# A basis chunk read as 32 KB in a row from each of 30 matrices, and a scratch laid out by row and type

## The reference

```
w = jnp.einsum('rb,bio->rio', att, basis)          # att [2, 30], basis [30, 512, 512] f32
for r in range(NUM_RELATIONS):
    gate = jax.nn.sigmoid(x_j @ gate_w[r, :, 0])
    msgs.append(gate[:, None] * x_j @ w[r])
msg = jnp.where((edge_type == 0)[:, None], msgs[0], msgs[1])
agg = jax.ops.segment_sum(msg, row, num_segments=x.shape[0])
return agg + x @ root + bias
```

## Time and profile before

| | us |
|---|---|
| median of 3 runs | 1989.06 |
| lowest and highest | 1987.30 and 1990.79 |
| the profiled execution, device time | 1988.88 |
| its span from first to last instruction | 1986.8 |

### The profile page before, as it was taken

The page is one execution under the profiler, slowest core; times in us unless marked ns, Lnnn a source line. Parts: engine busy times, 40 slices in busy tenths (PEclk is TensorE's granted clock), DMA queues, the critical chain, the costliest instruction groups (busy, mean ns, idle before and its releaser), DMA issues.

```text
span 1986.8 us, 23275 instructions
## 1 busy us (share of the span) xinstructions
PE 1867.5 (94%) x7728; PEld 891.8 (45%) x7728; DVE 798.5 (40%) x1918; ACT 625.1 (31%) x1200; POOL 8.0 (0%) x27
## 2 busy tenths in 40 slices
PE   5898886999999899999999999999999999977998
PEld 3555554633334344444444444454444444433443
DVE  7887775242111541110112223354544445483122
ACT  2555555146761241111111000132322323374000
POOL 1000000000000000000000000000000000000000
PEclk9999999799999779999999999999999999998999
DMA  7999988701000330100001111800000000021011
GB/s 186 266 251 254 238 214 248 286 1 38 1 0 1 132 153 0 43 1 1 21 0 43 43 32 34 337 0 6 22 6 22 6 22 17 6 74 48 21 53 43
DMA packets 46809, 157.52 MB, mean 79 GB/s; under 512 B 8747, under 2 KB 10691, under 8 KB 38247
## 3 DMA queue, kind: packets, MB, share of 16 engines
q1 hardware_dynamic: 42160, 142.27, 23.9%
q10 hardware_dynamic: 4534, 13.78, 1.9%
HBM read 120.38 MB, written 35.65 MB: 79 GB/s over the span
## 4 chain that ended last, share of the span: by engine, by line
PE 79%; DMA 7%; DVE 6%; issue 3%; DVEq 3%; ACT 2%; POOL 0%; ACTq 0%; POOLq 0%; SPq 0%
PE psum L1241 30%; PE psum L1227 30%; PE psum L1460 6%; DMA hs<-in_L_gnn_basis 3%; PE psum L1310 3%; PE psum L1363 2%; DMA adj<-in_L_gnn_basis 2%; PE psum L1411 2%; DMA hs<-in_L_gnn_Wim 2%; PE psum L1144 1%; PE psum L1165 1%; PE psum L1381 1%; DVE hs L597 1%; DVEq L585 1%; DVEq L598 1%
## 5 line engine op out<-in xcount | busy, mean ns | idle before, releaser
L1241 PE MATMUL psum<-hs,adj 128*128 128x512 f16 x2880 | 642.2, 380 | 0.8 <-DVE hs L722 0.8
L1227 PE MATMUL psum<-wb,xt 128*128 128x512 f32 x1152 | 508.9, 600 | 4.8 <-DVE hs L850 2.7
L1241 PEld LDWEIGHTS psum<-hs,adj 128*128 128x128 f16 x2880 | 279.8, 98 | 353.4 <-issue 36.2
L1227 PEld LDWEIGHTS psum<-wb,xt 128*128 128x128 f32 x1152 | 218.4, 192 | 272.9 <-issue 270.8
L1001 ACT ACTIVATE adj<-hs,pbias 128x512 f32<-128x512 f32 x216 | 134.5, 708 | 88.5 <-PE psum L1310 88.5
L1034 ACT ACTIVATE ua<-ua 128x512 f32<-128x512 f32 x60 | 37.8, 631 | 335.3 <-DVE ua L864 187.7
L801 DVE TENSOR_TENSOR vt<-psum,adj 128x512 f32<-128x512 f32 x24 | 16.6, 692 | 271.9 <-PE psum L1227 271.9
L1460 PE MATMUL psum<-hs,adj 128*128 128x512 f32 x288 | 123.8, 592 | 0.0
L1026 ACT ACTIVATE lnst<-lnst,bcol 128x1 f32<-128x1 f32 x36 | 10.6, 295 | 286.7 <-DVE lnst L781 283.4
L858 DVE SCALAR_TENSOR_TENSOR vt<-vt,scl,psum 128x512 f32<-128x512 f32 x60 | 44.8, 747 | 133.7 <-PE psum L1241 133.5
L849 DVE SCALAR_TENSOR_TENSOR vt<-psum,scl,hs 128x512 f32<-128x512 f32 x60 | 45.1, 751 | 122.0 <-ACT hs L1070 121.8
(11 more groups left out here) (223 smaller groups left out, 1891.2 us busy)
## 6 DMA issues: line engine op xcount, KB each, us to landing
hs<-in_L_gnn_basis SPq DMA_DIRECT2D x38, 960.0 KB, 12.1
adj<-in_L_gnn_basis SPq DMA_DIRECT2D x26, 960.0 KB, 14.8
aw_scratch<-xt ACTq DMA_DIRECT2D x12, 768.0 KB, 9.9
adj<-aw_scratch SPq DMA_DIRECT2D x1, 9216.0 KB, 35.9
x_scratch<-adj SPq DMA_DIRECT2D x24, 256.0 KB, 2.1
hs<-x_scratch SPq DMA_DIRECT2D x24, 256.0 KB, 2.6
ts_scratch<-adj SPq DMA_DIRECT2D x1, 4608.0 KB, 20.4
as_scratch<-adj SPq DMA_DIRECT2D x1, 4608.0 KB, 31.4
```

The costliest lines, as they stand in the source:

```text
L1227: x = pe.matmul(psum[:, bank, :], xt[:, i, k, :], w[:, k, :], start=first and k == 0, stop=last and k == 3)
L1241: x = pe.matmul(psum[:, i % 2 + (4 * half if own else 0), :], adj[:, m, j, P * i:P * i + P], hs[:, t, half, j, :], start=n == 1 or (own an ...
```

## The change

Five places change. The chunk's address: partition 4b + j now holds rows 16c + 4j to 16c + 4j + 3 of matrix b, so the four partitions of one matrix read 16 rows, 32 KB in a row, and the matrices are 1 MB apart. Before, the 120 partitions read 8 KB each at places 256 KB apart. The column order of attw: type t and quarter j are in column 2j + t instead of 4t + j (a stride of 2 in the output of the same four VectorE instructions). The scratch's shape: [512 rows, 2 types, 512] instead of [8, 128, 512]. The scratch write: the 8 partitions of one v, now in the order (j, t), go to four places of 4 KB (both types of one row) that are 16 KB apart, instead of eight places of 2 KB that are 256 KB apart. The read-back picks type t out of rows of 4 KB.

```diff
-        wc_dram = [nc.dram_tensor(f"comb{k}_scratch", [8, P, D], F32, kind="Internal").ap() for k in range(2)]
+        wc_dram = [nc.dram_tensor(f"comb{k}_scratch", [4 * P, 2, D], F32, kind="Internal").ap() for k in range(2)]
...
-        bases = [ins[f"L1_gnn_basis{l + 1}"].rearrange("b (j i) o -> (b j) (i o)", j=4) for l in range(2)]
-        combs = [wc_dram[l].rearrange("j (c q) o -> q j c o", q=4) for l in range(2)]
+        bases = [ins[f"L1_gnn_basis{l + 1}"].rearrange("b (c j i) o -> c b j (i o)", j=4, i=4) for l in range(2)]
+        combs = [wc_dram[l].rearrange("(c j q) t o -> c q j t o", j=4, q=4) for l in range(2)]
...
-                sp.dma_start(basis[basis_of(n)][0:120, :], bases[l][:, c * (4 * D):(c + 1) * (4 * D)]).then_inc(basis_in[basis_of(n)], 16)
+                sp.dma_start(basis[basis_of(n)][0:120, :], bases[l][c]).then_inc(basis_in[basis_of(n)], 16)
...
-                    sp.dma_start(combs[l][q, :, c, :], mixed[n % 4][32 * q:32 * q + 8, :]).then_inc(comb_out[n % 4], 16)
+                    sp.dma_start(combs[l][c, q], mixed[n % 4][32 * q:32 * q + 8, :]).then_inc(comb_out[n % 4], 16)
...
-                    sp.dma_start(wb[:, t, :, :], wc_dram[l][4 * t:4 * t + 4].rearrange("j p o -> p j o")).then_inc(weights["l1" + "ab"[l]], 16)
+                    sp.dma_start(wb[:, t, :, :], wc_dram[l].rearrange("(k p) t o -> t p k o", p=P)[t]).then_inc(weights["l1" + "ab"[l]], 16)
...
-                    x = dve.tensor_scalar(attw[0:120, l, 4 * t:4 * t + 4], attm[0:120, :], attc[0:120, l, t:t + 1], None, ALU.mult)
+                    x = dve.tensor_scalar(attw[0:120, l, t:8:2], attm[0:120, :], attc[0:120, l, t:t + 1], None, ALU.mult)
```

## The result

The changed kernel takes **2003.5 us** (median of 6 runs, 1999.7 to 2007.2), the kernel before 1991.6 (6 runs, 1987.3 to 1998.1; three of them are the runs shown ahead of the prediction). The ratio is 1.0052 with a 95% interval of 1.0033 to 1.0070: slower by some 10 us. The prediction, 1981 us, was to be faster by 8, so it has the wrong sign; its range, to 2004, holds the result by half a microsecond. The profiled execution took 1999.86 us, its span is 1997.7.

The account below looks back on a forecast made before the run. It took VectorE's pace, then late basis loads from about 150 us, to bound the building stage. Quicker loads gave -8 us, the other parts 0 or inside the 2 us left: 1988.88 to 1981 us, range 1977 to 2004.

Parts of the forecast that it names:

- What bounds the stage: Building stage, first 330 us: VectorE sets the pace until about 150 us, then late basis loads; at most 10 us to save.
- Step 1: Basis loads: new addresses, 32 KB in a row per matrix, are read faster, so fewer loads are late: -8 us.
- Step 2: Scratch writes: perhaps four engines instead of eight; 0 with quick loads, else 23 to 35 us more on these engines.
- part 1: Same as Step 1: the basis loads are read faster, -8 us.
- the third case: Same as The writes on four engines decide: scratch writes cost +8 to +35 us, taken at +12; chance 0.20.
- Step 3: SP's issuing of loads and scratch writes: at most 0.51 us each, SP busy 2.4 of 4.8 us; 0 to +2 us.
- SP case: SP's issuing becomes the bound from 1.1 us per scratch write; +50 us, 2039 us; chance 0.04.
- Step 4: Reading back the scratch, four loads of 1 MB in 2 KB pieces: nobody waits, cost 0, cover 28 us.
- The writes on four engines decide: Building stage: loads no quicker, scratch writes cost 0.36 to 0.54 us more per chunk; 2001 us, 1997 to 2024; chance 0.20.
- Nothing happens: Basis loads: engines stay in step, 2 MB apart, and read as slowly as before; 1989 us, within 4; chance 0.27.
- The reads get slower: Basis loads: matrices 1 MB apart read at a tenth less rate, 0.43 us per chunk, 28 over all; 2017 us; chance 0.04.

Follow-up runs that it names:

- the quick kernels: Kernel before with each basis load filling 128 partitions, 1 MB in a row (0.9953), or cut into partitions 0 to 111 and 112 to 119 (0.9949).
- the three delay runs: Kernel before with SP kept busy by semaphore increments: ten behind each load (0.9986), ten ahead of each load (0.9996), five behind each scratch write (1.0005).
- The cut at 112: Kernel before with each basis load issued as two transfers, partitions 0 to 111 and 112 to 119: 0.9949, 1981.8 us.

## Why the prediction was wrong, step by step

- **What bounds the stage** held. Late loads against VectorE's pace is what the floor of the quick kernels shows: "at most 10 us" to be won came out as 9.4 and 10.2 (0.9953 and 0.9949 of 1993 us). Of these the forecast took 8.
- **Step 1, the loads read faster (-8), failed.** It named "120 places of 8 KB, 256 KB apart" as what the slow loads have and the others haven't. But rows 8 and 9 differ from rows 7 in a second thing as well, the number of partitions: their transfers fill all 128, the basis loads 120. The prediction compared rows that differ in two things and chose the one that the change touches. The contiguous read into 120 partitions (15.2 GB/s) and into 128 (23.7) settle it. So the sentence that rows 7 against rows 8 agree with a slow pitch does not hold either. In place of -8 the new loads gave +3 to +6 us (1.0028, 1.0016).
- **Step 2, the writes on four engines**: the count came true (1025 small packets fewer, 1020 forecast). "0 if part 1 comes true" held too, 0.9957 against 0.9953 with quick loads. With slow loads the third case asked +8 to +35 and took +12; measured are 1.0012 and 1.0021, **2 to 4 us**. The engines' rate was not the hard limit that the sum took: in the changed kernel a busy engine gave 16.1 instead of 15.1 GB/s, with the new writes alone 16.0. That this made the cost small is argued, as it is not known what raised the rate.
- **Step 3, SP's issuing**, was sized too low: 0.51 us at most for either, measured 0.58 per write and 0.91 per load; the nearest rows, loads of the scratch with equal shapes, were no bound. SP is busy 3.4 us of a chunk, not 2.4. The lateness was under-rated too: SP was late for 17 of 60 loads, where the forecast had some of the last ten. That it is covered held as far as it was tried: the three delay runs show no cost of either half of it, and both halves together were not run. The SP case (from 1.1 us per write) was far.
- **Step 4**, reading back: landing 5.0/6.2/7.4 us and, as said, no wait of TensorE or ScalarE for it.
- **The cases.** "The writes on four engines decide", 0.20, comes nearest: 2001 forecast, 2003.5 measured, and waits from 91 us on, its sign. But only some 3 of the 10 us are its own, so that the time it names was met by luck. "Nothing happens" had the right view of the rate (still 15 to 16) and the wrong reason. "The reads get slower" got its sign only: not a lower rate, no 28 us.
- **Open** is what the new loads cost. It is not their addresses in the sense of places and pitch, as those of old shape show. The trace has their issue 0.58 us longer and the quickest landing at 7.7 to 8.1 us instead of 6.6. About a microsecond at each load that is waited for would give 3 to 6 us over the run; that is argued, not shown, since the one run with the new shape and other places (1.0011) lies between none and all of it, and the second trace of the new loads has the long issue and no more waits than the kernel before. Open too is whether the long issues of loads and writes cost more together than apart.

The cut at 112 is the version that beats both: 1981.8 us, 0.9949 of the kernel before, one more issue of 0.32 us per chunk.

## What to carry to other kernels

Before putting a slow transfer down to its addresses, divide its bytes by busy engine time and lay it beside a transfer that differs in one thing only; here the number of partitions mattered and the addresses did not. Count how many pieces the fullest DMA engine carries: the cut that gives it nine instead of eight took 1.2% longer here. The count does not tell the good cut (112) from the idle one (64), so try a few cuts of a transfer that doesn't fill all partitions; each costs one issue. See also whether the issuing engine still stands ready when a buffer comes free. A nicer layout in DRAM can cost more than it gives where it makes the shapes of both sides unequal: longer issues, fewer engines.

## What the runs showed of the hardware that was not expected

- Into 120 partitions a busy DMA engine moved 14.8 to 15.2 GB/s whether it read 960 KB in a row or 8 KB pieces 248 or 256 KB apart; into 128 it moved 23.7, into 112 18.1, and into 64 14.3 with hardly any load in flight beside another.
- A cut at partition 112 gave 0.9949, at 64 1.0006, at 104 1.0124, the same bytes each time.
- SP's issue of a DMA took 0.30 us (8 x 512), 0.33 (120 x 2048), 0.58 (4 x 2 x 512 from 8 partitions) and 0.88 to 0.91 (30 x 4 x 2048 into 120), the medians of 128 and 38 issues; loads cut at partition 64 took 0.52 to 0.56, cut at 112 0.32.
- Single runs of one kernel differ more than its ratio: the run with delays behind the writes has a median of 1992.5 us and a profiled execution of 1981.1, with 4 waits for a load instead of 12. So the counts of waits of one trace, above, say less than the ratios.
- With scratch writes of 0.58 us and loads of 0.91 us SP was late for 17 of 60 loads; with 0.30 and 0.33 for one.
